# A graph layer with 5 engine programs: the loop over pairs of row blocks is written out as straight code

## The reference

```python
bw = jnp.sign(weight)
ba = jnp.maximum(jnp.sign(x), 0.0)
xw = ba @ bw.T                        # 8192 x 256, small whole numbers
out = jax.nn.relu(adj @ xw)           # adj is 268 MB and is read once
y = x + out
result = (y - mean(y)) / sqrt(var(y) + 1e-5)   # over the last axis
```

## Time and profile before

| | |
|---|---|
| time, median of 3 runs | 1066.31 us |
| fastest and slowest run | 1064.25 and 1069.69 us |
| span of the profiled execution | 1064.2 us |
| mean granted TensorE clock | 0.976 |
| PE busy | 993.5 us (93%) |
| DVE busy | 858.2 us (81%) |
| POOL busy | 840.3 us (79%) |
| ACT busy | 605.2 us (57%) |
| moved by DMA | 294.36 MB, mean 277 GB/s |

### The profile page before, as it was taken

How to read it: one execution, slowest core, us unless ns; L and a number is a source line. 1 busy time by engine, 2 the same in 40 slices (tenths; PEclk the granted TensorE clock), 3 DMA queues, 4 the chain that set the end, 5 groups by cost and what they waited for, 6 DMA issues and landing times.

```text
span 1064.2 us, 15065 instructions
## 1 busy us (share of the span) xinstructions
PE 993.5 (93%) x4484; PEld 812.8 (76%) x4484; DVE 858.2 (81%) x881; ACT 605.2 (57%) x647; POOL 840.3 (79%) x361
## 2 busy tenths in 40 slices
PE   5578699999998999899998999899998999999996
PEld 4356578888877888788886888778886888888885
DVE  4656489898959989598886989599895989799893
ACT  3345366666546656466565665466564665566562
POOL 0346489899868988599896998599885998889893
PEclk9889899999999999999999999989999999999999
DMA  9999999999998999899998999999998999999961
GB/s 216 226 223 224 228 286 320 302 332 317 308 315 241 292 324 282 250 295 311 299 297 250 300 313 294 290 236 289 327 284 253 300 306 299 300 290 297 309 198 39
DMA packets 313166, 294.36 MB, mean 277 GB/s; under 512 B 9760, under 2 KB 313120, under 8 KB 313120
## 3 DMA queue, kind: packets, MB, share of 16 engines
q1 hardware_dynamic: 186400, 168.06, 62.3%
q10 hardware_dynamic: 126720, 125.84, 42.3%
HBM read 285.47 MB, written 8.39 MB: 276 GB/s over the span
## 4 chain that ended last, share of the span: by engine, by line
PE 44%; POOL 26%; issue 12%; SPq 9%; DMA 4%; DVE 3%; ACT 1%; POOLq 0%; ACTq 0%
PE ps L619 44%; POOL lo L299 26%; SPq L217 7%; DMA raw<-in_adj_dram 4%; SPq L205 2%; DVE turned L450 1%; DVE lo L456 1%; PE ps L644 1%; DVE ps L450 0%; ACT hi L326 0%; DVE relu L414 0%; DVE stats L464 0%; POOLq L298 0%; SPq L195 0%; ACT rows L344 0%
## 5 line engine op out<-in xcount | busy, mean ns | idle before, releaser
L299 POOL TENSOR_TENSOR lo<-turned,hi 128x1024 fp32r<-128x1024 f32 x352 | 839.2, 2413 | 207.1 <-ACT hi L326 203.9
L619 PE MATMUL ps<-hi,xw 128*128 128x512 f32 x2048 | 810.0, 396 | 31.8 <-DVE lo L456 27.1
L619 PE MATMUL ps<-lo,xw 128*128 128x512 f32 x2048 | 804.8, 393 | 0.0
L326 ACT ACTIVATE hi<-turned 128x1024 fp32r<-128x1024 f32 x352 | 373.4, 1061 | 281.4 <-DVE turned L450 161.7
L619 PEld LDWEIGHTS ps<-hi,xw 128*128 128x128 f32 x2048 | 389.6, 190 | 120.0 <-DVE lo L456 24.9
L619 PEld LDWEIGHTS ps<-lo,xw 128*128 128x128 f32 x2048 | 389.4, 190 | 80.4
L450 DVE STREAM_TRANSPOSE turned<-raw 128x1024 f32<-128x1024 f32 x352 | 426.1, 1218 | 22.3 <-DMA raw<-in_adj_dram 22.3
L456 DVE TENSOR_TENSOR lo<-ps,hi 128x1024 fp32r<-128x1024 f32 x160 | 194.8, 1217 | 128.1 <-ACT hi L326 127.5
L326 ACT ACTIVATE hi<-ps 128x1024 fp32r<-128x1024 f32 x160 | 164.1, 1025 | 134.4 <-issue 58.9
L450 DVE STREAM_TRANSPOSE ps<-raw 128x1024 f32<-128x1024 f32 x160 | 195.1, 1219 | 18.6 <-DMA raw<-in_adj_dram 18.6
L344 ACT ACTIVATE rows<-rows,shift,rstd 128x256 f32<-128x256 f32 x62 | 36.4, 588 | 0.0
(11 more groups left out here) (23 smaller groups left out, 47.8 us busy)
## 6 DMA issues: line engine op xcount, KB each, us to landing
raw<-in_adj_dram ACTq DMA_DIRECT2D x240, 512.0 KB, 10.4
raw<-in_adj_dram SPq DMA_DIRECT2D x240, 512.0 KB, 9.0
raw<-in_adj_dram SPq DMA_DIRECT2D x64, 256.0 KB, 7.4
x_sb<-in_x_dram SPq DMA_DIRECT2D x32, 256.0 KB, 8.1
rows<-in_x_dram SPq DMA_DIRECT2D x16, 512.0 KB, 8.8
out_dram<-rows SPq DMA_DIRECT2D x15, 512.0 KB, 13.7
out_dram<-rows SPq DMA_DIRECT2D x2, 256.0 KB, 2.3
rows<-in_L_gnn_weight_dram SPq DMA_DIRECT2D x1, 256.0 KB, 3.7
```

What stands on the lines that cost most here:

```text
L299: pool.tensor_tensor(lo[:, s], turned[:, t], hi[:, s].bitcast(f32), ALU.subtract).then_inc(p_los_made, 1)
L326: act.activation(hi[:, s], src, ACT.Copy).then_inc(his_made, 1)
L619: return pe.matmul(acc[h][a], xw[:, step, a * P:(a + 1) * P], part[:, s, k * MB:(k + 1) * MB], start=(step == 0 and part is hi), stop=(ste ...
```

## The change

The loops are replaced by Python loops, which write out all eight pairs one behind the other, on every engine. The index is then a plain number: the loop's branch, the register arithmetic and the address registers fall away, and every wait compares with a constant. Nothing else is changed: the operations, their tiles and their order on each engine stay, and the numbers of transfers too.

```diff
@@ sync
-            with sp.Fori(1, PAIRS) as q:
+            for q in range(1, PAIRS):
                 for h in range(2):
                     load_block(q, h)
@@ gpsimd
-            pair(0)
-            with pool.Fori(1, PAIRS) as q:
+            for q in range(PAIRS):
                 pair(q)
@@ scalar
-            pair(0)
-            with act.Fori(1, PAIRS - 1) as q:
+            for q in range(PAIRS):
                 pair(q)
-
-            pair(PAIRS - 1)
             make_relu(PAIRS - 1, 1)
@@ vector
-            pair(0)
-            with dve.Fori(1, PAIRS) as q:
+            for q in range(PAIRS):
                 pair(q)
@@ tensor
-            pair(0)
-            with pe.Fori(1, PAIRS) as q:
+            for q in range(PAIRS):
                 pair(q)
```

## The result

The changed kernel takes 1034.49 us (median of 4 runs, 1032.98 to 1038.44) against 1067.20 us before (4 runs, 1064.25 to 1069.69). The ratio is 0.9703, with a 95% interval of 0.9675 to 0.9730: a gain of 31.7 us at the ratio, where 29.3 was forecast.

What follows compares the result with a forecast made beforehand. PE was taken to bound nearly everywhere, interrupted five times by ACT's stall. Removing 29.3 us takes the span from 1064.2 to 1034.9 us; adding 2.1 us for the median gives 1037 us, range 1032 to 1047.

Steps and rivals of the forecast that it cites:

- ACT's stall at five returns: At ACT's loop branch into pairs 2 to 6: idle on "issue", 11.4 us at most, all five removed by the change.
- It is a fetch of code: At ACT's taken loop branch: its target lies outside the two blocks held, so ACT waits for instructions, 11.39 us.
- two fetches in a row, 5.6 us each: ACT's stall at a loop return, if made of two successive code fetches: one uncovered fetch costs half, 5.6 us.
- ACT's body is the only one that does not fit: ACT's loop body, 310 instructions a pair, was claimed alone to exceed its engine's instruction window; DVE's has 200.
- The floor of 117.88 us a pair: PE's uninterrupted time per pair, from matmuls and turning blocks back; pairs 2 to 6 would each fall to it.
- The cover of 7.4 us: At pair boundaries: PE stands still only if ACT idles longer than 7.4 us; 4.4 us would leave 3.0.
- New code costs nothing: Instruction fetches of the written-out code, mainly PE's: costed at nothing, upper bound 134 us; late PE code had 4% chance.
- the 24 more that were counted on: Extra packets expected on PE's instruction queue q8: 4 blocks a pair in six pairs.
- Register arithmetic at nothing: Small loop instructions removed per pair, about 140 on ACT, 90 DVE, 45 POOL, 70 PE: costed at nothing.
- The sum: Pairs 2 to 6 fall from 618.66 to 589.4 us together, a gain of 29.3 us.
- Transfers have room, but little: DMA transfers throughout: a pair needs 302 GB/s, pair 1 moved 315, so 4% of shown room.
- this rival: Transfers set the pace: at 289 GB/s no gain, 1066 us; at 295, 1054 us; chance 7%.

Runs made afterwards that it cites:

- slot 212: Kernel before, all loops kept, ACT's loop body moved to begin at instruction 212 of a 256-instruction block: 1154.36 us, ratio 1.0805.
- slots 0 and 196: Kernel before, all loops kept, ACT's loop body moved to begin at instruction 0 or 196 of a 256-instruction block: 1036.81 us and 1035.57 us.
- 254: Kernel before, all loops kept, ACT's loop body aligned to begin two instructions before a 256-instruction block's end: 1066.54 us, ratio 0.9991.

## Why the prediction was right

- *ACT's stall at five returns is the loss.* Right. Writing out ACT alone gives the whole gain and writing out the others none.
- *It is a fetch of code.* This was argued from the rule for a window of two blocks and from one coincidence of sizes; it is shown now. The same instructions cost 0 or 11 us at a return by their address alone, the hint for the branch removes the stall, DVE can be given it, and two packets of q14 lie in it. The guess of two fetches in a row, 5.6 us each, fits: the packets stand 5.2 us apart, and one late fetch gave 6.4 us in all at slot 212, two gave 11.
- *ACT's body is the only one that does not fit.* Wrong as it was argued, and luck that it did no harm. By the prediction's own rule an engine holds two blocks of 256, 512 instructions, and the body has 310: by its size it fits. It stalled for where it began; at slots 0 and 196 the same body returns free. What carried the forecast was the stall that the trace showed on ACT, not the count.
- *The floor of 117.88 us a pair.* Right to the second decimal: 117.90 in the profile after.
- *The cover of 7.4 us.* Borne out: 4.4 and 6.4 us on ACT left PE without a wait at the return, 11 us did not. At 6.4 us the pair still took 118.97 us, 1.1 more than the floor.
- *New code costs nothing.* Right: q8 went from 10 to 35 packets, in the full change and in the kernel where it brings no gain, without a microsecond. Of the 24 more that were counted on, 25 came.
- *Register arithmetic at nothing.* Right within what the runs tell: ACT alone at 0.9710 and everything at 0.9703 have overlapping intervals.
- *The sum.* Five pairs gave the 29.3 us. From span to span it is 27.6, since the beginning of the run profiled after was 1.7 us later; from median to median it is 32.7. The times of both kernels spread by some 5 us from run to run. I take that to be the beginning, which waits for transfers, and the difference to lie in it; with one run of each profiled, it is not shown.
- *Transfers have room, but little.* Right for this change, which runs at 305 GB/s with no wait of DVE after 200 us. The kernel at slot 212 shows that the room can be lost at a stroke. I had priced this rival between 1037 and 1066; when it came, it cost 1154. I had taken the 289 GB/s of the pairs with a stall for the lowest rate that it could fall to, and it fell to 236.

## What to carry to other kernels

Idle time put down to "issue" just behind a loop's branch, on one engine and not on the others, is likely a code fetch. See whether an instruction queue has packets in it, and look at where the body begins before unrolling anything: bodies of 310 and 400 instructions stalled here at a bad place, and one of 310 did not at two good ones. One placed loop head, or the hint for the branch, gave here nearly what writing out 5 programs gave. Do not place by guess, though: slot 212 cost 87 us over the kernel before, sixteen instructions from a slot that gained 31. Price such a stall at the engine that bounds, and against the wait that would stand in its place anyway: some 11 us on ACT were 5.9 us on PE.

## What the runs showed of the hardware that I had not expected

Code stays usable over a branch backwards. The body at slots 196 to 506 returned five times without a packet on q14 from 300 to 900 us, and PE's body of over 1,100 instructions was never fetched again (10 packets on q8, the last in pair 1). The Trainium skill (Runtime: NRT & Kernel Launch, Instruction fetch mechanics) calls the memory a FIFO with purely sequential prefetch, and has a taken branch wait for a fetch if its target lies outside a window of two blocks; that a body within it returns free is what the runs add.

ACT's code seems to come in smaller pieces than 256 instructions. In the kernel with only ACT written out, 900 instructions of ACT run from the packet of q14 at 370.8 us to the seventh after it, at 972.7: some 129 for each packet, of 8 KB. On PE a packet has 16 KB. By pieces of 128 the bodies at slots 0 and 196 lie over three, those at 212 and 254 over four, so the four placements do not tell the two sizes apart. But the body at slot 212 lies over three blocks of 256 and, with the hint, stayed held; as four pieces of 128 it would fill just what two blocks hold. That is a reading, and was not tested.

Two queues moved more than one. In the first 60 us the same transfers went at 298 GB/s from SP and ACT against 222 from SP alone. The Trainium skill (Trainium Kernel Development and Optimization, Key Constraints) says that issuing from several engines only saves issue time; here the measurement says otherwise. SP's time for issuing them (1.1 us by the median for a transfer of 256 KB, up to 3.6) may be part of it, but the packets of its one queue already filled 111.5% of the 16 engines' time in these 60 us, which does not look like engines left waiting for work.

This kernel has a second, much slower pace of transfers: 236 to 258 GB/s with the DMA share at 1.11, as at 305. A refetch that held ACT for some 6.4 us at each round was enough to bring it about, and the kernel never found its way back. In it SP takes 3.5 us to issue a transfer.
